# A graph network with two residual norms on one core: loads, split order and product order at both ends changed

## The chip, the cores and the metric

One core of one Trainium2 chip. The metric is the device time of one execution in microseconds (us); lower is better.

## The reference

16 independent batches, each with node features x (512 x 256) and a weighted adjacency adj (512 x 512), all float32:

```python
x = layernorm(x + (adj @ (x @ W0 + b0)) / adj.sum(-1))
y = relu(adj @ (x @ W1) + b1)
y = relu(adj @ (y @ W2) + b2)
out = layernorm(x + adj @ (y @ W3) + b3)
```

The kernel moves b0 behind the division (row sums cancel), so it adds b0 to x ahead of the first sum.

## The kernel before, in words

**Precision.** TensorE works on float32r. Every operand is split in two: `hi` is a rounded copy (by ScalarE, `copy_hi`, line 424), `lo` is full minus hi (by VectorE, `sub_hi`, line 596, or by GpSimd, lines 789, 797, 804). A product is three passes, hi*hi, hi*lo, lo*hi, accumulated in one PSUM bank (`three_passes`, lines 166 to 168). VectorE and ScalarE read the banks; GpSimd reads SBUF alone.

**Tiles.** T = 4 tiles of 128 nodes, KF = 2 halves of 128 features. Eight products make a batch: p0 = x W0 (h), p1 = adj h, then norm1 gives x1; p2 = adj x1 (g, transposed), p3 = g W1 and relu (x2), p4 = x2 W2 (s2), p5 = adj s2 and relu (x3), p6 = x3 W3 (s3), p7 = adj s3, then norm2 gives y and the store. p0, p1, p4, p6 and p7 work tile by tile on 256 columns, p2, p3 and p5 on 512. Four banks are called bank_b (p0, p1, p6, p7), four bank_a.

**Order.** Each engine has its program written out by hand, and semaphores tie them together. An engine runs its own program in order, so what is queued behind a waiting instruction waits too. TensorE interleaves two batches: `step(new)` runs p5(old), p2(new), p6(old), p3(new), p7(old), p0(nxt), p4(new), p1(nxt). The first batch, FIRST, and the first products of `second` stand ahead of the loop; the last step is written out behind it (lines 408 to 419), as LAST and `old`.

**Start.** SyncE's queue (SP) issues every load: w0, xT of batch 0 in two halves, adj of batch 0 in two halves, x, b0; then line 192 waits until both halves of xT are split, because the second batch's xT goes into the same buffer `xT_raw`; then adj of batch 1 in two halves (into `adj_rows`, free then), w1, and behind a wait for xb (line 197) x of batch 1 and the rest. ScalarE's own program for the start is lines 544 to 578, VectorE's 721 to 754, GpSimd's 816 to 829. GpSimd adds b0 to x (`add_b0`, xb), then splits adj of `second`. p1(second) waits for all four h_lo and all four adj_lo of its batch (lines 304, 305). 18 products on zeros (`warm_up`) run before the first load lands.

**End.** VectorE's `norm2(old)` makes, for tile a, v = bank + x1b, its statistics, and for tile a - 1 the reciprocal deviation and y; its first turn waits, at line 685, until the store of the batch before is complete, since `y` is one buffer. `stored` counts 16 for each store. SP stores the last but one batch with line 224 when all its four y are ready, and the last batch tile by tile with line 228.

Of the kernel before, what the change touches and what calls it, by code (L numbers as in the profile page):

```python
# [10 lines left out]
P = 128  # L11
# [8 lines left out]
def build(nc, xT, x, adjT, adj, w0, w1, w2, w3, b0, b1, b2, b3, out):  # L20
# [8 lines left out]
    with ExitStack() as ctx:  # L29
# [7 lines left out]
        xT_raw = sb("xT_raw", [P, T, KF, P], F32)  # L37
# [24 lines left out]
        xT_hi, xT_lo = pair("xT", [P, T, KF, P])  # L62
# [32 lines left out]
        adj1_loaded = [sem(f"adj1_half{n}_loaded") for n in range(2)]  # L95
        rows_loaded = sem("rows_loaded")
# [75 lines left out]

        block = ctx.enter_context(nc.Block())

        @block.sync
        def _(sp):
# [6 lines left out]
            halves = [half_of(half, T) for half in range(2)]  # L183
# [21 lines left out]
            def load(i):  # L205
# [6 lines left out]
                sp.dma_start(xT_raw[:, :], xT[i]).then_inc(xT_loaded, DMA)  # L212
# [19 lines left out]
        def _(pe):  # L232
# [11 lines left out]

            def p0(nxt, reader, read, banks=bank_b):
# [8 lines left out]
                xw_product(p0_done, banks, (lambda k, j: xT_hi[:, j, k, :], lambda k, j: xT_lo[:, j, k, :]), 0, ready)  # L254
# [515 lines left out]
        def _(pool):  # L770
# [98 lines left out]
```

## Time and profile before

| | us |
|---|---|
| three runs: median (lowest, highest) | 555.73 (554.92, 555.89) |
| the profiled execution's own time | 556.23 |
| its span, first to last instruction | 554.4 |
| warm-up products | 1.19 to 4.86 |
| first product of p0 | 5.19 |
| first product of the loop's first step, p5(FIRST) | 43.85 |
| last product of p7(LAST) starts | 549.57 |
| last store issued | 552.18 |

Mean granted TensorE clock over the span 0.996; the core's loads and stores move 58.23 MB at a mean of 105 GB/s, but 316 GB/s between 5 and 10 us. The profile gives for each instruction its start and length from the span's start, and, where its engine was idle before it, for how long and what released it. "x2" joins instructions of one kind: the length is then that of the pair, from the first's start to the last's end.

### The profile page before, as it was taken

Reading aid. Unit: us, or ns where it says so; the run is one execution under the profiler, and the core shown is the slowest. Engines: PE = TensorE matmul, PEld = TensorE weight load, DVE = VectorE, ACT = ScalarE, POOL = GpSimd, SP = SyncE. Lnnn points to the kernel's source line nnn. Section 1 sums busy time; section 2 is a strip of 40 time slices with the busy share of each in tenths; the row PEclk is TensorE's granted clock in tenths of the full one; section 3 lists DMA queues with packets and bytes.
Section 4 is the critical chain, followed back from the end, with each engine's and each line's share of the span. In section 5 each row is a group of like instructions: output and inputs, shape, how many; then the busy total and the mean of one; then the engine's idle time right before and its main releaser. Section 6 shows DMA issues by size and latency. Waiting matters only on the chain.

```text
span 554.4 us, 10623 instructions
## 1 busy us (share of the span) xinstructions
PE 540.8 (98%) x3666; PEld 498.8 (90%) x3666; DVE 350.6 (63%) x1034; ACT 307.5 (55%) x757; POOL 207.6 (37%) x223
## 2 busy tenths in 40 slices
PE   7799999999999999999999999999999999999996
PEld 6778999989899898999989899898999989899885
DVE  5774665756657475665756657475665757657455
ACT  4456646566554756655566554746655566553632
POOL 1745409062260804408062260804408062261000
PEclk9899999999999999999999999999999999999999
DMA  7730070511507033070612507043070612500002
GB/s 248 250 128 2 1 267 1 215 53 59 208 0 264 1 121 144 4 260 0 207 57 61 204 0 265 0 136 129 9 256 0 217 49 63 204 2 39 1 1 77
DMA packets 15286, 58.23 MB, mean 105 GB/s; under 512 B 1952, under 2 KB 2720, under 8 KB 13472
## 3 DMA queue, kind: packets, MB, share of 16 engines
q1 hardware_dynamic: 15264, 57.94, 29.1%
q8 instruction: 13, 0.21, 0.2%
q14 instruction: 9, 0.07, 0.0%
HBM read 49.55 MB, written 8.39 MB: 104 GB/s over the span
## 4 chain that ended last, share of the span: by engine, by line
PE 93%; DVE 3%; DMA 2%; ACT 1%; issue 0%; SPq 0%; DVEq 0%
PE bank_a L166 16%; PE bank_a L167 16%; PE bank_a L168 16%; PE bank_b L166 15%; PE bank_b L167 15%; PE bank_b L168 15%; DMA xT_raw<-in_xT 2%; DVE xT_lo L596 0%; DVE x_lo L596 0%; DVE v L645 0%; DVE x L652 0%; DVE stats L656 0%; DVE h_lo L596 0%; ACT x_hi L500 0%; ACT xT_hi L424 0%
## 5 line engine op out<-in xcount | busy, mean ns | idle before, releaser
L797 POOL TENSOR_TENSOR adj_lo<-adj_raw,adj_hi 128x512 fp32r<-128x512 f32 x56 | 70.8, 1299 | 272.5 <-ACT adj_hi L424 272.5
L596 DVE TENSOR_TENSOR x_lo<-bank_a,x_hi 128x512 fp32r<-128x512 f32 x64 | 44.3, 692 | 69.8 <-ACT bank_a L502 69.8
L166 PE MATMUL bank_b<-h_hi,adj_hi 128*128 128x256 f32 (+1 forms) x256 | 72.0, 281 | 3.8 <-DVE h_lo L596 2.6
L166 PE MATMUL bank_b<-s_hi,adj_hi 128*128 128x256 f32 x256 | 71.8, 280 | 0.9 <-DVE s_lo L596 0.9
L167 PE MATMUL bank_b<-h_lo,adj_hi 128*128 128x256 f32 (+1 forms) x256 | 71.8, 280 | 0.0
L477 ACT ACTIVATE std<-moments,eps_col 128x1 f32<-128x1 f32 x64 | 18.9, 295 | 95.2 <-DVE moments L664 95.2
L168 PE MATMUL bank_b<-h_hi,adj_lo 128*128 128x256 f32 (+1 forms) x256 | 71.6, 279 | 0.0
L167 PE MATMUL bank_b<-s_lo,adj_hi 128*128 128x256 f32 x256 | 71.4, 279 | 0.0
L168 PE MATMUL bank_b<-s_hi,adj_lo 128*128 128x256 f32 x256 | 71.4, 279 | 0.0
L500 ACT ACTIVATE x_hi<-bank_a,b_col 128x512 fp32r<-128x512 f32 x64 | 43.8, 684 | 22.4 <-PE bank_a L168 20.9
L784 POOL TENSOR_TENSOR x1b<-x,b_all 128x256 f32<-128x256 f32 x64 | 46.2, 763 | 17.4 <-DVE x L652 17.4
L166 PEld LDWEIGHTS bank_b<-h_hi,adj_hi 128*128 128x128 f32 x256 | 48.3, 189 | 4.6 <-DVE h_lo L596 2.8
L778 POOL TENSOR_TENSOR xb<-x_raw,b_all 128x256 f32<-128x256 f32 x64 | 47.0, 776 | 13.0 <-DMA b_all<-in_b 11.6
L166 PE MATMUL bank_a<-adj_hi,x_hi 128*128 128x512 f32 x128 | 50.6, 395 | 0.2 <-DVE x_lo L596 0.2
L167 PE MATMUL bank_a<-adj_lo,x_hi 128*128 128x512 f32 x128 | 50.3, 393 | 0.0
L168 PE MATMUL bank_a<-adj_hi,x_lo 128*128 128x512 f32 x128 | 50.2, 392 | 0.0
L521 ACT ACTIVATE std<-moments,eps_col 128x1 f32<-128x1 f32 x64 | 18.9, 295 | 56.2 <-DVE moments L704 56.2
L167 PE MATMUL bank_a<-adj_lo,s_hi 128*128 128x512 f32 x128 | 49.9, 390 | 0.0
L166 PE MATMUL bank_a<-adj_hi,s_hi 128*128 128x512 f32 x128 | 49.9, 390 | 0.0
L168 PE MATMUL bank_a<-adj_hi,s_lo 128*128 128x512 f32 x128 | 49.9, 389 | 0.0
L166 PEld LDWEIGHTS bank_b<-s_hi,adj_hi 128*128 128x128 f32 x256 | 48.1, 188 | 1.8 <-DVE s_lo L596 1.1
L167 PEld LDWEIGHTS bank_b<-s_lo,adj_hi 128*128 128x128 f32 x256 | 47.9, 187 | 0.7
(95 smaller groups left out, 1596.8 us busy)
## 6 DMA issues: line engine op xcount, KB each, us to landing
adj_raw<-in_adjT SPq DMA_DIRECT2D x30, 512.0 KB, 5.6
adj_rows<-in_adj SPq DMA_DIRECT2D x14, 1024.0 KB, 9.4
x_raw<-in_x SPq DMA_DIRECT2D x16, 512.0 KB, 7.4
xT_raw<-in_xT SPq DMA_DIRECT2D x15, 512.0 KB, 6.6
out_y<-y SPq DMA_DIRECT2D x15, 512.0 KB, 2.9
w_raw<-in_w SPq DMA_DIRECT2D x4, 256.0 KB, 5.0
adj_rows<-in_adjT SPq DMA_DIRECT2D x2, 512.0 KB, 7.8
xT_raw<-in_xT SPq DMA_DIRECT2D x2, 256.0 KB, 4.3
```

The source lines that it names most:

```text
L166: pe.matmul(acc, st[0], mv[0], start=start, stop=False)
L167: pe.matmul(acc, st[0], mv[1], start=False, stop=False)
L168: return pe.matmul(acc, st[1], mv[0], start=False, stop=stop)
L477: act.activation(std1[:, j:j + 1], moments1[:, j, 1:2], ACT.Sqrt, bias=eps_col[:, :]).then_inc(std1_ready, 1)
L500: act.activation(hi[:, f, :], bank_a[f][:, :], ACT.Relu, bias=bias[:, f:f + 1])
L521: act.activation(std2[:, j:j + 1], moments2[:, j, 1:2], ACT.Sqrt, bias=eps_col[:, :]).then_inc(std2_ready, 1)
L596: return dve.tensor_tensor(lo, full, hi.bitcast(F32), ALU.subtract)
L778: pool.tensor_tensor(xb[:, j, :], x_raw[:, j, :], b0_all[:, :], ALU.add).then_inc(xb_ready, 1)
L784: pool.tensor_tensor(x1b[:, slot(batch), j, :], x1[:, j, :], b3_all[:, :], ALU.add).then_inc(x1b_ready, 1)
L797: pool.tensor_tensor(adj_lo[:, s, k, :], raw[:, k, :], adj_hi[:, s, k, :].bitcast(F32), ALU.subtract).then_inc(adj_split, 1)
```

## The change

Start:
- ScalarE's queue issues the four adj transfers of batches 0 and 1, at the head of its program; SP keeps the rest.
- xT and x of batch 1 go into the buffers `y` and `v2`, so SP's waits of lines 192 and 197 are gone. `xT_raw` is laid out as [P, T, F], the same bytes in the same order.
- adj of batch 0 is split by two engines: GpSimd takes k = 0 and 2, VectorE 1 and 3.
- ScalarE's, VectorE's and GpSimd's orders are changed to fit: norm1(FIRST, tile 0) stands ahead of both splits of the second xT on VectorE.

End:
- TensorE's order is p3, p7(old, 0 and 1), p4, p5, p7(old, 2), p6, p7(old, 3), p7. p7(old, 2) and (old, 3) write bank_a. `p6_last` runs the half k = 0 over all four tiles, then k = 1.
- s3 of LAST goes into the buffers of h, so that p7(old) can still read s3 of `old`.
- GpSimd makes y of tiles 0 to 2 of LAST. Line 685's wait stays as it is, and GpSimd has the same one.

The diff, cut to its core:

```diff
             sp.dma_start(w_raw[:, 0, :, :], w0).then_inc(w_loaded[0], DMA)
-            for half, tiles in enumerate(halves):
-                sp.dma_start(xT_raw[:, tiles], xT[0, :, tiles]).then_inc(xT0_loaded[half], DMA)
-            for half, tiles in enumerate(halves):
-                sp.dma_start(adj_raw[:, tiles, :], adjT[0, :, tiles, :]).then_inc(adj_loaded[half], DMA)
+            for half in range(2):
+                tiles = half_of(half, T)
+                sp.dma_start(xT_raw[:, tiles, :], xT[0, :, tiles, :]).then_inc(xT0_loaded[half], DMA)
             sp.dma_start(x_raw[:, :, :], x[0]).then_inc(x_loaded, DMA)
             sp.dma_start(b0_all[:, :], b0.partition_broadcast(P)).then_inc(b_loaded[0], DMA)
-
-            sp.wait_ge(xT_split, 2)
-            sp.dma_start(xT_raw[:, :], xT[1]).then_inc(xT_loaded, DMA)
-            for half, tiles in enumerate(halves):
-                sp.dma_start(adj1_raw[:, tiles, :], adjT[1, :, tiles, :]).then_inc(adj1_loaded[half], DMA)
+            sp.dma_start(xT1_raw[:, :, :], xT[1]).then_inc(xT_loaded, DMA)
             sp.dma_start(w_raw[:, 1, :, :], w1).then_inc(w_loaded[1], DMA)
-            sp.wait_ge(xb_ready, T)
-            sp.dma_start(x_raw[:, :, :], x[1]).then_inc(x_loaded, DMA)
+            sp.dma_start(x1_raw[:, :, :], x[1]).then_inc(x1_loaded, DMA)
...
@@ TensorE
-                pe.wait_ge(s2_split, at(old, T, T))
                 adj_product_T(old, p5_done, bank_a[0:2], (s2_hi, s2_lo), s2_split)
...
+            def p6_last(old):
+                for k in range(KF):
+                    pe.wait_ge(x3_split, at(LAST, KF, k + 1))
+                    for j in range(T):
+                        cols = slice(j * P, (j + 1) * P)
+                        if k == 0 and j < T // 2:
+                            pe.wait_ge(v2_ready, at(old, T, j + 1))
+                        mm = three_passes(pe, bank_b[j][:, 0:F], (x3_hi[:, k, cols], x3_lo[:, k, cols]),
+                                          (w_hi[:, 3, k, :], w_lo[:, 3, k, :]), k == 0, k == KF - 1)
+                        if k == KF - 1:
+                            mm.then_inc(p6_done, 1)
...
             p4(LAST)
-            p7(old, range(2, 3))
             p5(LAST)
-            p7(old, range(3, T))
-            p6(LAST, v2_ready, old)
+            p7(old, range(2, 3), bank_a)
+            p6_last(old)
+            p7(old, range(3, T), bank_a)
             p7(LAST)
@@ ScalarE
+            for batch, raw, loaded in ((0, adj_raw, adj_loaded), (1, adj1_raw, adj1_loaded)):
+                for half in range(2):
+                    tiles = slice(half * T // 2, (half + 1) * T // 2)
+                    act.dma_start(raw[:, tiles, :], adjT[batch, :, tiles, :]).then_inc(loaded[half], DMA)
             act.wait_ge(eps_set, 1)
             act.activation(sqrt_eps[:, :], eps_col[:, :], ACT.Sqrt)
             split_xT(FIRST, 0)
+            split_adj(FIRST, 0)
             split_xT(FIRST, 1)
+            split_adj(FIRST, 1)
             h(FIRST, tiles=range(0, 2))
-            split_adj(FIRST, 0)
-            split_adj(FIRST, 1)
-            h(FIRST, tiles=range(2, T))
             split_adj(FIRST, 2)
             split_adj(FIRST, 3)
+            h(FIRST, tiles=range(2, T))
+            split_adj(second, 0)
+            split_adj(second, 1)
             split_xT(second, 0)
             split_xT(second, 1)
-            split_adj(second, 0)
-            split_adj(second, 1)
             norm1(FIRST, None, range(0, 1))
...
             s2(LAST)
-            norm2(before(LAST), range(2, 3))
             x3(LAST, 0)
             x3(LAST, 1)
+            norm2(before(LAST), range(2, 3))
+            s3(LAST)
             norm2(before(LAST), range(3, T))
-            s3(LAST)
             norm2(LAST)
@@ VectorE
             split_xT(FIRST, 0)
             split_xT(FIRST, 1)
+            split_adj0(1)
             h(FIRST, tiles=range(0, 2))
-            split_adj(FIRST, 0)
-            split_adj(FIRST, 1)
+            split_adj0(3)
             h(FIRST, tiles=range(2, T))
-            split_adj(FIRST, 2)
-            split_adj(FIRST, 3)
+            norm1(FIRST, range(0, 1))
             split_xT(second, 0)
-            norm1(FIRST, range(0, 1))
             split_xT(second, 1)
             norm1(FIRST, range(1, 2))
...
             s2(LAST)
-            norm2(before(LAST), range(2, 3))
             x3(LAST, 0)
             x3(LAST, 1)
-            norm2(before(LAST), range(3, T + 1))
+            norm2(before(LAST), range(2, 3), bank_a)
             s3(LAST)
+            norm2(before(LAST), range(3, T + 1), bank_a)
             norm2(LAST)
@@ GpSimd
+            for k in range(0, T, 2):
+                pool.wait_ge(adj_hi_ready, k + 1)
+                pool.tensor_tensor(adj_lo[:, 0, k, :], adj_raw[:, k, :], adj_hi[:, 0, k, :].bitcast(F32),
+                                   ALU.subtract).then_inc(adj0_even_split, 1)
             pool.wait_ge(b_loaded[0], DMA)
             add_b0(FIRST)
...
+            pool.wait_ge(stored, at(LAST, DMA, DMA))
+            for j in range(T - 1):
+                pool.wait_ge(rstd2_ready, at(LAST, T, j + 1))
+                pool.tensor_scalar(y[:, j, :], v2[:, j, :], moments2[:, j, 0:1], rstd2[:, j:j + 1],
+                                   ALU.subtract, ALU.mult).then_inc(y_last_ready, 1)
```

## Rows read from the trace of the kernel before

**Rows 1.** The page, busy time of each engine (share of the span)
```profile
PE 540.8 (98%) x3666; PEld 498.8 (90%) x3666; DVE 350.6 (63%) x1034; ACT 307.5 (55%) x757; POOL 207.6 (37%) x223
```

**Rows 2.** Stretches: length; busy PE, PEld, DVE, ACT, POOL; clock; DMA share; GB/s
```profile
20.00:25.00 5.00, 2.36 (x19) 2.17 (x18) 3.92 (x13) 1.69 (x6) 5.00 (x6) 0.96 0.73 219
25.00:30.00 5.00, 4.84 (x16) 3.62 (x16) 4.29 (x13) 2.14 (x6) 3.62 (x5) 0.70 0.80 289
```

**Rows 3.** TensorE's timeline at the start: start, length, instruction, [idle before <-releaser]
```profile
1.19 3.67 PE L260 MATMUL bank_a<-zeros 128*128 128x256 f32 x18 [1.19 <-DVE zeros L721]
...
10.71 0.36 PE L166 MATMUL bank_b<-h_hi,adj_hi 128*128 128x258 f32 x1 [0.76 <-DVE adj_lo L596]
...
23.48 0.39 PE L166 MATMUL bank_b<-h_hi,adj_hi 128*128 128x258 f32 x1 [2.64 <-DVE h_lo L596]
```

**Rows 4.** VectorE's timeline at the start
```profile
15.89 0.69 DVE L596 TENSOR_TENSOR xT_lo<-xT_raw,xT_hi 128x512 fp32r<-128x512 f32 x1 [2.31 <-ACT xT_hi L424]
16.50 0.16 DVE L635 RECIPROCAL inv_rows<-bank_b 128x1 f32<-128x1 f32 x1
...
17.93 1.22 DVE L596 TENSOR_TENSOR xT_lo<-xT_raw,xT_hi 128x512 fp32r<-128x512 f32 x1
```

**Rows 5.** ScalarE's timeline at the start
```profile
7.35 0.63 ACT L424 ACTIVATE xT_hi<-xT_raw 128x512 fp32r<-128x512 f32 x1 [2.31 <-DMA xT_raw<-in_xT]
...
9.21 1.15 ACT L424 ACTIVATE adj_hi<-adj_raw 128x512 fp32r<-128x512 f32 x2 [0.68 <-DMA adj_raw<-in_adjT]
10.27 0.64 ACT L424 ACTIVATE h_hi<-bank_b 128x256 fp32r<-128x256 f32 x2
```

**Rows 6.** TensorE's timeline at the end
```profile
530.95 0.28 PE L166 MATMUL bank_b<-s_hi,adj_hi 128*128 128x256 f32 x1
...
539.99 0.38 PE L166 MATMUL bank_b<-w_hi,x_hi 128*128 128x256 f32 x1 [0.64 <-DVE x_lo L596]
...
543.93 0.39 PE L166 MATMUL bank_b<-s_hi,adj_hi 128*128 128x256 f32 x1 [0.93 <-DVE s_lo L596]
```

**Rows 7.** VectorE's timeline at the end
```profile
527.47 0.42 DVE L688 TENSOR_TENSOR v<-bank_b,x1b 128x256 f32<-128x256 f32 x1
...
528.55 0.39 DVE L688 TENSOR_TENSOR v<-bank_b,x1b 128x256 f32<-128x256 f32 x1
...
530.53 1.46 DVE L596 TENSOR_TENSOR s_lo<-bank_a,s_hi 128x256 fp32r<-128x256 f32 x4 [0.64 <-ACT s_hi L424]
...
545.75 0.42 DVE L688 TENSOR_TENSOR v<-bank_b,x1b 128x256 f32<-128x256 f32 x1 [1.87 <-PE bank_b L168]
...
549.89 0.42 DVE L688 TENSOR_TENSOR v<-bank_b,x1b 128x256 f32<-128x256 f32 x1
...
551.74 0.41 DVE L698 TENSOR_SCALAR y<-v,moments,rstd 128x256 f32<-128x256 f32 x1
```

**Rows 8.** GpSimd's timeline at the start
```profile
12.08 3.50 POOL L778 TENSOR_TENSOR xb<-x_raw,b_all 128x256 f32<-128x256 f32 x4 [11.62 <-DMA b_all<-in_b]
17.30 5.50 POOL L797 TENSOR_TENSOR adj_lo<-adj_rows,adj_hi 128x512 fp32r<-128x512 f32 x4 [1.72 <-ACT adj_hi L424]
```

**Rows 9.** Issues of w0 and x0: size each, us from issue to landing; SyncE's timeline
```profile
w_raw<-in_w SPq DMA_DIRECT2D x1, 256.0 KB, 2.8
...
3.21 0.43 SPq L189 DMA_DIRECT2D x_raw<-in_x  x1
...
x_raw<-in_x SPq DMA_DIRECT2D x1, 512.0 KB, 8.5
```

**Rows 10.** Table of half microseconds at the start
```profile
2.50:3.00 0.50, 0.50 (x4) 0.50 (x4) 0.00 (x0) 0.00 (x0) 0.00 (x0) 1.00 0.95 356
4.50:5.00 0.50, 0.37 (x4) 0.16 (x2) 0.32 (x1) 0.50 (x1) 0.00 (x0) 1.00 1.10 119
```

**Rows 11.** SyncE's timeline and the DMA issues at the end
```profile
542.14 0.35 SPq L224 DMA_DIRECT2D out_y<-y  x1
...
out_y<-y SPq DMA_DIRECT2D x1, 512.0 KB, 2.6
```

More of the change, by code:

```diff
@@ L60, in build @@
         std1 = sb("std1", [P, T], F32)
-        xT_hi, xT_lo = pair("xT", [P, T, KF, P])
+        xT_hi, xT_lo = pair("xT", [P, T, F])
         g_hi, g_lo = pair("g", [P, KF, N])
@@ L171, in build @@
         adj1_raw = adj_rows
+        xT1_raw, x1_raw = y, v2
+        s3_last_hi, s3_last_lo = h_hi[:, :, 0:F], h_lo[:, :, 0:F]
         block = ctx.enter_context(nc.Block())
@@ L252, in ready @@
                         pe.wait_ge(reader, at(read, T, j + 1))
-                xw_product(p0_done, banks, (lambda k, j: xT_hi[:, j, k, :], lambda k, j: xT_lo[:, j, k, :]), 0, ready)
+                xw_product(p0_done, banks, (features(xT_hi), features(xT_lo)), 0, ready)
             def warm_up():
@@ L360, in p6, with p7 @@
                            lambda j: pe.wait_ge(reader, at(read, T, j + 1)))
-            def p7(old, tiles=range(T)):
+            def p6_last(old):
[9 more added lines that the diff above has]
+                            mm.then_inc(p6_done, 1)
+            def p7(old, tiles=range(T), banks=bank_b):
                 pe.wait_ge(s3_split, at(old, T, T))
+                hi, lo = (s3_last_hi, s3_last_lo) if old is LAST else (s3_hi, s3_lo)
                 s = slot(old)
@@ L600, in split_xT, with split_adj0 @@
                 dve.wait_ge(xT_hi_ready, at(nxt, 2, half + 1))
-                sub_hi(xT_lo[:, tiles], xT_raw[:, tiles], xT_hi[:, tiles]).then_inc(xT_split, 1)
-            def split_adj(nxt, k):
-                s = slot(nxt)
-                dve.wait_ge(adj_hi_ready, at(nxt, T, k + 1))
-                sub_hi(adj_lo[:, s, k, :], adj_raw[:, k, :], adj_hi[:, s, k, :]).then_inc(adj_split, 1)
+                raw = xT1_raw if nxt is second else xT_raw
+                sub_hi(xT_lo[:, tiles, :], raw[:, tiles, :], xT_hi[:, tiles, :]).then_inc(xT_split, 1)
+            def split_adj0(k):
+                dve.wait_ge(adj_hi_ready, k + 1)
+                sub_hi(adj_lo[:, 0, k, :], adj_raw[:, k, :], adj_hi[:, 0, k, :]).then_inc(adj_split, 2)
             def h(new, banks=bank_b, tiles=range(T)):
@@ L676, in x3, with norm2 @@
                 sub_hi(x3_lo[:, f, :], bank_a[f][:, :], x3_hi[:, f, :]).then_inc(x3_split, 1)
-            def norm2(old, turns=range(T + 1)):
+            def norm2(old, turns=range(T + 1), banks=bank_b):
                 for j in turns:
@@ L695, in norm2 @@
                         dve.bn_stats(stats2[:, a, :], v2[:, a, :]).then_inc(stats2_ready, 1)
-                    if b >= 0:
+                    if b >= 0 and (old is not LAST or b == T - 1):
                         dve.wait_ge(rstd2_ready, at(old, T, b + 1))
@@ L771, in add_b0 @@
             def add_b0(batch):
-                pool.wait_ge(x_loaded, at(batch, DMA, DMA))
+                if batch is FIRST:
+                    pool.wait_ge(x_loaded, DMA)
+                elif batch is second:
+                    pool.wait_ge(x1_loaded, DMA)
+                else:
+                    pool.wait_ge(x_loaded, at(batch, DMA, 0))
+                raw = x1_raw if batch is second else x_raw
                 for j in range(T):
@@ L848 @@
     arrays = {
[L849 removed]
+        "xT": x.reshape(NB, P, T, KF, P).transpose(0, 4, 2, 3, 1).reshape(NB, P, T, F),
         "x": x.reshape(NB, P, T, F),
```

46 lines of the change are left out of this document (29 added, 17 removed).

## The prediction

> **What bounds the kernel now.** The page's first part says TensorE: busy 98% of the span [rows 1]. In the middle nothing else can be bought, because TensorE has no gaps there, and the change leaves the loop alone. So I looked for the idle 2% where the change works, at the two ends, first in the table of stretches, then in TensorE's timeline with the idle time before each instruction.
>
> At the start TensorE is busy 2.36 of the 5 us from 20 to 25, and in the next 5 us it is "busy" but at a mean clock of 0.70 [rows 2]. The timeline has the main hole: 2.64 us before 23.48, the first product of the second batch's p1, released by the h_lo split on VectorE [rows 3]. The first p1 starts at 10.71, after 0.76 us of waiting. Following VectorE back from 23.48: it stood 2.31 us until 15.89 for the second batch's xT, which could only be loaded after the first had been split, although p1 of tile 0 was long done; then come norm1 from 16.50 and the second xT split at 17.93, which takes 1.22 us beside a busy GpSimd against 0.69 us for the same shape without one [rows 4]. From VectorE's 16.50 to TensorE's 23.48 it is one chain, 6.98 us. Before it lies the landing of the first xT's second half: ScalarE starts on it at 7.35 [rows 5].
>
> At the end TensorE stands 0.64 us before p6(LAST), for x3's split, and 0.93 us before p7(LAST), for s3's [rows 6]. Then a tail: the last v starts at 549.89, the last y at 551.74 and ends at 552.15 [rows 7], then the last store.
>
> **Start, part by part.** I count everything from L, the moment ScalarE gets xT's second half (7.35 now), because ScalarE runs in order and has that split ahead of split_adj(1) and h.
>
> ScalarE after L: xT_hi, adj_hi 1, h_hi 0 and 1. A pair of adj_hi took 1.15 us and a pair of h_hi 0.64 [rows 5], so adj_hi 1 ends at L+1.15 and h_hi 1 at L+1.8. VectorE: xT_lo to L+1.35, adj_lo 1 to L+1.95, h_lo 0 and 1 (0.37 each) to L+2.7. p1 starts at L+2.75; now it is L+3.36. k=0 and 1 are 12 products of 0.12 us, to L+4.2. For k=2 VectorE first has adj_lo 3, which now has GpSimd's adj_lo 2 beside it, so 1.22 us, then h_lo 2: L+4.5. p1 of tile 0 is done and seen at L+5.9, and norm1(FIRST, 0) can start, since xT1 no longer stands ahead of it. That replaces 16.50. The rest is the chain of 6.98 us plus one more xT split of 1.13 us (both now lie behind norm1). So p1(second) starts at L+14.0; now it is L+16.1. **The new order is worth 2.1 us if L does not move.** Behind it VectorE's chain to x_lo carries p2_first as today, so I let the 2.1 us through whole. Removing the halves of the clock (0.50 in part of that 0.70 stretch) brings nothing of itself: p2 waits for x_lo then.
>
> GpSimd must not be the new end: adj_lo 0 and 2 at about 1.3 us each, done by L+3.7; then four xb in 3.5 and four adj_lo in 5.5 [rows 8], to L+12.7, under L+14.0, if b0 has landed by L+5. Loads of w1, w2, w3 and x1 come earlier on SP; nobody waits on them. Four issues on ScalarE's queue cost it 4 x 0.43 us, before anything is there to split: hidden by the first xT's landing (4.4 now), and the table load moves behind them under the same cover. The other format of xT changes no run of bytes: a partition still reads one contiguous piece.
>
> **But L moves.** Today w0 and both xT halves, 0.79 MB, are first in one queue; w0 lands 2.8 us after its issue [rows 9]. Now four adj transfers of 0.52 MB are issued on a second queue from 0.75 us on, before or beside w0. No row shows two queues in flight, so I bound it. Lower end: xT keeps its place, L = 7.35, no cost. Upper end: the two queues alternate transfer by transfer at today's pace. Then 2.36 MB go by before xT's second half is in (adj 0.52, w0 0.26, adj 0.52, xT 0.26, adj 0.52, xT 0.26). Exactly 2.36 MB go by today up to x0, and x0, issued at 3.21, takes 8.5 us, landing at 11.7 [rows 9]: L later by 4.4. Between them: today's pace contains poor half-microseconds (119 GB/s at 4.5) beside good ones (356 GB/s at 2.5) [rows 10], and a second queue may fill the poor ones. 2.36 MB at 356 are 6.6 us, from first bytes at about 2.0, and w0 shows 0.9 us from its last byte to its landing: 9.5, so L later by 2.2. I take this value: alternation seems the natural thing for two queues on the same engines, and today's stalls look like waiting rather than limit. **Start: -2.1 + 2.2 = +0.1** (from -2.1 to +2.3).
>
> The Trainium skill, "DMA: Bandwidth & Descriptors", in "Queues, rings and completion order", says that each engine takes turns between its queue rows, a packet at a time, and its rules for authors say that spreading transfers over SP, ACT and GpSimd gives no bandwidth. That speaks against this half of the change, and by it alone the upper bound, alternation at an unchanged pace, would be the sum; no run here shows it.
>
> **End, part by part.** p7(old, 2) at 530.95 is moved behind p5(LAST). s2's splits run from 530.53 at 0.37 us each [rows 6, 7], so p5 starts at 531.0 without a hole. x3 is then split 1.3 us earlier (538.6) while p7(old, 2) and the first half of p6_last (12 + 12 products) keep TensorE busy to 539.2; p7(old, 3) covers s3's split (12 products, 1.41 us, against 1.1). Both holes go: 0.64 and 0.93, and 0.1 each because the product behind a hole takes 0.39 and not 0.28. p7(LAST) starts at 542.1 instead of 543.93, **1.8 us earlier for TensorE**. Other banks (bank_a 2 and 3) are free by then.
>
> What is queued behind? norm2(old, 3) now comes after p7(old, 3), at 542.1. v to y is one chain of 2.26 us (549.89 to 552.15), so with 0.3 us from product to v, y of the last but one batch is whole at 544.65. Today its store is issued at 542.14 [rows 11]. That store took 2.6 us, so it lands at 547.3 instead of 544.7. And norm2(LAST), line 685, waits for `stored` before its first v. Today that v comes at 545.75, held by TensorE, with the store in already. **Now it is held by the store, 1.5 us later than today.** Then VectorE works through four turns that TensorE has ready: 527.47 to 528.55 is 1.08 us a turn, with rstd in it about 1.16, where today TensorE paces them at 1.42. The last v starts at 550.8 against 549.89; the last y saves 0.15 because y 2 is on GpSimd. **End: +0.75** (from +0.4 to +1.0). GpSimd's tensor_scalar has no row; by its 128x256 tensor_tensor (0.8 us) y 2 is done at 552.0, before VectorE's y 3 at 552.9, and hidden; at twice that it would still be level.
>
> **Sum.** +0.1 + 0.75 = +0.85. The profiled execution took 556.23 (span 554.4, 1.8 around it); the median is 555.73, so I subtract 0.5: 555.73 + 0.85 = 556.6. A measurement of this kernel can tell about 0.2%, 1.1 us, from no change.
>
> **Rivals.**
> 1. *xT is not delayed.* For: ScalarE's first issue may come late (behind its table load, 1.28 us), and SP's three transfers are small. Against: adj's are issued within the same microsecond. -2.1 + 0.75 = -1.35, 554.4. Decides if L stays below 7.8. Chance 0.22.
> 2. *Strict alternation at today's pace.* +2.3 + 0.75 = +3.05, 558.8: slower. For: 2.36 MB have a landing today. The taking of turns that the Trainium skill describes in "DMA: Bandwidth & Descriptors" would be this case. Chance 0.2.
> 3. *The clock falls early.* The warm-up ends at 4.86 [rows 3]; if xT comes late, TensorE idles about 3 us, and today 2.64 us of idle is followed by the level 1.2 GHz [rows 2, 3]. Half speed under p1_first costs up to 1.5 us more: 558.1. Chance 0.12.
> 4. *The wait for the store does not bind* (y whole earlier than I count): -1.8 and +0.1 give 554.0, with rival 1 551.8. Against: the order of VectorE's program is fixed. Chance 0.08.
> The forecast keeps 0.38.
>
> **Numbers.** Faster by over 0.2%: most of rivals 1 and 4, 0.27. Slower: rivals 2 and 3 and some of the forecast's upper side, 0.41. Within: 0.32. The range holds rivals 1 and 2 and half of 4's spread: 553.6 to 559.2. The forecast's own range is 555.6 to 557.8.
>
> **What would show it.** Right: xT's second half landing near 9.5; VectorE's norm1 ahead of the second xT split; p1(second) about 14 us after L; no idle before p6 and p7(LAST); VectorE's first v of LAST waiting for out_y's DMA, and turns of 1.1 us behind it. Wrong: xT landing at 7.3 or 11.7, a clock of 0.5 before 15 us, GpSimd's adj_lo releasing p1(second), or v of LAST released by TensorE.

## The result: slower, and the profile after

| | before | after |
|---|---|---|
| median (lowest, highest), us | 555.33 (554.91, 555.89) | 560.0 (559.36, 560.46) |
| span of the profiled execution | 554.4 | 558.3 |
| mean granted clock | 0.996 | 0.991 |
| ScalarE takes xT's second half (L) | 7.35 | 10.90 |
| p1(second) starts | 23.48 | 26.07 |
| p7(LAST) starts | 543.93 | 544.77 |
| first v of LAST | 545.75 | 549.99 |
| last y ends | 552.15 | 555.66 |

The ratio of after to before is 1.008, 95% interval 1.0065 to 1.0096. The forecast was 556.6, range 553.6 to 559.2: the sign it gave most weight to was right, the size was not. Between the two profiled executions the span grows by 3.9 us: the start brings 2.6 and the end the rest. The medians are 4.7 us apart, because the profiled execution of the kernel before (556.23) was 0.9 above its median and that of the kernel after (560.09) only 0.1 above its own.

The first part of the page after, which answers to [rows 1]: the busy times hardly moved, so the change is in what lies between the instructions.

```profile
PE 541.0 (97%) x3666; PEld 500.4 (90%) x3666; DVE 349.7 (63%) x1029; ACT 307.0 (55%) x757; POOL 213.8 (38%) x228
```

**Start.** ScalarE's timeline after (its own DMA issues, then what it split) answers to [rows 5]:

```profile
0.74 0.87 ACTq L571 DMA_DIRECT2D adj_raw<-in_adjT  x2
1.64 1.29 ACTq L571 DMA_DIRECT2D adj_rows<-in_adjT  x2
...
8.97 0.63 ACT L446 ACTIVATE xT_hi<-xT_raw 128x512 fp32r<-128x512 f32 x1 [4.51 <-DMA xT_raw<-in_xT]
...
10.90 0.63 ACT L446 ACTIVATE xT_hi<-xT_raw 128x512 fp32r<-128x512 f32 x1 [0.78 <-DMA xT_raw<-in_xT]
```

adj is issued at 0.74, ahead of w0 at 0.87 on SyncE's queue, and both halves of xT are waited for: L is 10.90, 3.55 us later. The table of stretches shows what the memory gave meanwhile (columns as in [rows 2], which are of later stretches):

```profile
2.00:3.00 1.00, 1.00 (x6) 1.00 (x6) 0.00 (x0) 0.04 (x1) 0.00 (x0) 1.00 0.84 193
3.00:4.00 1.00, 1.00 (x7) 1.00 (x6) 0.00 (x0) 1.00 (x1) 0.00 (x0) 1.00 0.89 250
...
5.00:6.00 1.00, 0.41 (x2) 0.11 (x1) 0.00 (x0) 0.00 (x0) 0.00 (x0) 1.00 1.04 414
```

The two queues reach 414 GB/s together, but only from 5 us on; from 2 to 4 us there were 193 and 250. The profile's DMA view parts the queues (q1 is SyncE's, q10 ScalarE's; packets, MB, share of the 16 engines), here from 3.0 to 3.4, from 3.4 to 3.9 and from 5 to 8 us:

```profile
q10 hardware_dynamic: 23, 0.09, 75.4%
...
q10 hardware_dynamic: 30, 0.12, 94.4%
q1 hardware_dynamic: 8, 0.02, 8.4%
...
q10 hardware_dynamic: 224, 0.84, 72.4%
q1 hardware_dynamic: 189, 0.35, 30.6%
```

Until 3.5 us only adj's queue moved anything, although w0 had been issued at 0.87. From then on the two took packets in about equal numbers (364 on SyncE's queue and 342 on ScalarE's from 4 to 9 us), but SyncE's packets were about half as large here, so w0 and xT got 0.68 MB in that time and adj 1.21. VectorE and TensorE then, against [rows 3] and [rows 4]:

```profile
6.22 0.43 DVE L760 CAST w_hi<-w_raw 128x512 fp32r<-128x512 f32 x1 [4.93 <-DMA w_raw<-in_w]
...
17.30 0.17 DVE L665 RECIPROCAL inv_rows<-bank_b 128x1 f32<-128x1 f32 x1 [1.12 <-PE bank_b L171]
...
18.73 3.01 DVE L624 TENSOR_TENSOR xT_lo<-y,xT_hi 128x512 fp32r<-128x512 f32 x2
...
24.60 1.42 DVE L624 TENSOR_TENSOR h_lo<-bank_a,h_hi 128x256 fp32r<-128x256 f32 x4 [0.94 <-ACT h_hi L446]
```

```profile
9.74 0.77 PE L274 MATMUL bank_b<-w_hi,xT_hi 128*128 128x256 f32 x2 [4.34 <-ACT xT_hi L446]
...
15.90 0.39 PE L169 MATMUL bank_b<-h_hi,adj_hi 128*128 128x258 f32 x1 [0.43 <-DVE h_lo L624]
...
26.07 0.46 PE L169 MATMUL bank_b<-h_hi,adj_hi 128*128 128x258 f32 x1 [2.60 <-DVE h_lo L624]
```

norm1(FIRST, 0) is at L+6.4 where it was at L+9.15, so the order did what it says. But the hole before p1(second) is as wide as before (2.60 for 2.64), and both splits of the second xT, 3.01 us, now stand in the chain ahead of it. Counted from L, p1(second) came at 15.17 where it came at 16.1.

**End.** TensorE's two holes of [rows 6] are gone, and p7(LAST) starts at 544.77, which is the forecast's 542.1 and the start's delay of 2.6:

```profile
540.68 0.28 PE L169 MATMUL bank_b<-w_hi,x_hi 128*128 128x256 f32 x1
...
544.77 0.34 PE L169 MATMUL bank_b<-h_hi,adj_hi 128*128 128x256 f32 x1
```

What stands in their place is in VectorE's, GpSimd's and SyncE's timelines, against [rows 7] and [rows 11]:

```profile
546.83 0.41 DVE L729 TENSOR_SCALAR y<-v,moments,rstd 128x256 f32<-128x256 f32 x1
549.99 0.42 DVE L718 TENSOR_TENSOR v<-bank_b,x1b 128x256 f32<-128x256 f32 x1 [2.76 <-DMA out_y<-y]
...
551.08 0.39 DVE L718 TENSOR_TENSOR v<-bank_b,x1b 128x256 f32<-128x256 f32 x1
...
555.13 0.53 DVE L729 TENSOR_SCALAR y<-v,moments,rstd 128x256 f32<-128x256 f32 x1
```

```profile
551.88 3.63 POOL L879 TENSOR_SCALAR y<-v,moments,rstd 128x256 f32<-128x256 f32 x3 [34.22 <-DVE rstd L722]
```

```profile
547.26 0.35 SPq L224 DMA_DIRECT2D out_y<-y  x1
553.13 3.21 SPq L231 DMA_DIRECT2D out_y<-y  x4
```

VectorE stands 2.76 us for the store of the last but one batch, which is issued when its y is whole. While it stands, TensorE runs ahead: the four turns behind it are VectorE's own, 1.1 us apart. GpSimd's three y take 1.2 us each, end at 555.51, 0.15 before VectorE's last, and so leave two stores to issue behind the end in place of one.

### The profile page after: what moved, and what is told of

Read it like the earlier page. It is cut to its first block, busy times and chain, and to the rows that moved or that the text cites. A ratio compares the mean times of both kernels' runs of the same rounds, so it can differ in the third digit from the quotient of the medians.

```text
span 558.3 us, 10616 instructions
## 1 busy us (share of the span) xinstructions
PE 541.0 (97%) x3666; PEld 500.4 (90%) x3666; DVE 349.7 (63%) x1029; ACT 307.0 (55%) x757; POOL 213.8 (38%) x228
## 4 chain that ended last, share of the span: by engine, by line
PE 91%; DVE 3%; DMA 2%; issue 1%; ACT 1%; POOL 1%; SPq 0%; DVEq 0%; POOLq 0%
PE bank_a L169 16%; PE bank_a L171 16%; PE bank_a L170 16%; PE bank_b L169 15%; PE bank_b L170 15%; PE bank_b L171 15%; DMA xT_raw<-in_xT 1%; DVE xT_lo L624 1%; DMA out_y<-y 0%; POOL adj_lo L853 0%; DVE v L675 0%; DVE x L682 0%; DVE stats L725 0%; POOL xb L813 0%; DVE x_lo L624 0%
## 5 line engine op out<-in xcount | busy, mean ns | idle before, releaser
L169 PE MATMUL bank_b<-h_hi,adj_hi 128*128 128x256 f32 (+1 forms) x272 | 76.7, 282 | 3.0 <-DVE h_lo L624 3.0
L170 PE MATMUL bank_b<-h_lo,adj_hi 128*128 128x256 f32 (+1 forms) x272 | 76.6, 282 | 0.0
L171 PE MATMUL bank_b<-h_hi,adj_lo 128*128 128x256 f32 (+1 forms) x272 | 76.3, 281 | 0.0
L169 PE MATMUL bank_b<-s_hi,adj_hi 128*128 128x256 f32 x232 | 65.0, 280 | 0.0
L170 PE MATMUL bank_b<-s_lo,adj_hi 128*128 128x256 f32 x232 | 64.7, 279 | 0.0
L171 PE MATMUL bank_b<-s_hi,adj_lo 128*128 128x256 f32 x232 | 64.7, 279 | 0.0
L169 PEld LDWEIGHTS bank_b<-h_hi,adj_hi 128*128 128x128 f32 x272 | 51.6, 190 | 3.5 <-DVE h_lo L624 3.4
L170 PEld LDWEIGHTS bank_b<-h_lo,adj_hi 128*128 128x128 f32 x272 | 51.6, 190 | 0.1
L171 PEld LDWEIGHTS bank_b<-h_hi,adj_lo 128*128 128x128 f32 x272 | 51.6, 190 | 0.0
L624 DVE TENSOR_TENSOR g_lo<-bank_a,g_hi 128x512 fp32r<-128x512 f32 x32 | 22.1, 692 | 40.2 <-ACT g_hi L446 40.2
```

What stands on the lines that cost most here:

```text
L169: pe.matmul(acc, st[0], mv[0], start=start, stop=False)
L170: pe.matmul(acc, st[0], mv[1], start=False, stop=False)
L171: return pe.matmul(acc, st[1], mv[0], start=False, stop=stop)
L624: return dve.tensor_tensor(lo, full, hi.bitcast(F32), ALU.subtract)
```

## The experiments

Every run is compared with the kernel before on the same chip; the kernel before had medians of 554.8 to 555.4 there, with single executions from 553.5 to 557.6. Its first loads land at varying times: in four profiled executions with its order of loads ScalarE took xT's second half at 7.35, 6.33, 7.10 and 6.53, and in the three of them with its whole start p1(second) came at 23.48, 22.50 and 22.68. So the profiled execution of the kernel before is a late one. In the six traces with all of adj on ScalarE's queue, L was 10.85 to 11.15 each time.

### Each end by itself

The changed start with the end of before, and the reverse: the parts of the diff swapped whole.

> The start of the change, with the end of the kernel before (order of products, banks, all y on VectorE, each line as before). Theory (the delayed xT at the start costs 2.6 us and passes whole to the end, the end costs 1.3 more): p1 of the second batch starts at 26.1 as in the changed kernel, p7 of the last batch at 546.6 (543.93 + 2.6), span 557.0, ratio 1.0047. Rival (the loop absorbs part of the late start, and the loss lies in the end): p7 of the last batch before 545.5, span near 555.5.

> The start of the kernel before, with the end of the change. Theory (the wait for the last but one store takes the place of the two holes): p1 of the second batch at 23.5, p7 of the last batch at 542.1, first v of the last batch at 547.3, released by the store's DMA, last y done at 553.0, and one more issue of 0.35 us on SyncE's queue behind GpSimd's y 2: span 555.7, ratio 1.0023. Rival (the holes taken away reach the end): first v released by TensorE at 543.9, last y done at 550.3, span 552.6.

The start alone: 558.25, ratio 1.0061 (1.0035 to 1.0087), span 557.2, p1(second) at 26.08 and p7(LAST) at 546.69, as the theory had it: the loop absorbs nothing of the late start. The end alone: 557.48, ratio 1.0039 (1.002 to 1.0058). Its profiled execution had an early start (p1(second) at 22.50, span 554.6), so its end is read from there. VectorE:

```profile
546.27 0.42 DVE L709 TENSOR_TENSOR v<-bank_b,x1b 128x256 f32<-128x256 f32 x1 [2.74 <-DMA out_y<-y]
...
551.40 0.53 DVE L720 TENSOR_SCALAR y<-v,moments,rstd 128x256 f32<-128x256 f32 x1
```

With 0.98 added to bring p1(second) to 23.48, the last y ends at 552.9, 0.76 later than in the kernel before: the forecast's +0.75. Both ends cost, and their sum, 1.0%, agrees with the whole, 0.8%, within the intervals. The ratio of the end alone is larger than its expected 1.0023, which is still inside its interval.

### The end: the wait for the store, and GpSimd's y

The y of LAST goes into the buffer v1, and VectorE and GpSimd no longer wait for the store (cut to its core):

```diff
+        y_last = v1
...
-                sp.dma_start(out[NB - 1, :, j, :], y[:, j, :]).then_inc(stored, DMA)
+                sp.dma_start(out[NB - 1, :, j, :], y_last[:, j, :]).then_inc(stored, DMA)
...
-                        dve.wait_ge(stored, at(old, DMA, DMA))
+                        if old is not LAST:
+                            dve.wait_ge(stored, at(old, DMA, DMA))
...
-            pool.wait_ge(stored, at(LAST, DMA, DMA))
```

> The changed kernel with y of the last batch written into the buffer v1, which is dead by then, so that nothing of the last batch waits for the store of the batch before; GpSimd still makes y 0 to 2. Theory (that wait costs the end): first v of the last batch at 546.5, released by TensorE; last v at 550.75, last y done at 553.0, span 555.9, 2.4 us under the changed kernel. Rival (GpSimd's y at 1.2 us each is the other bound): y 2 comes from GpSimd behind VectorE's y 3, and the span falls by less than 1.5 us.

556.51, ratio 1.0035 (1.0016 to 1.0054), span 555.4, 2.9 below the changed kernel's, with p1(second) at 26.13. The first v of LAST follows VectorE's last y of `old` at once:

```profile
547.18 0.42 DVE L721 TENSOR_TENSOR v<-bank_b,x1b 128x256 f32<-128x256 f32 x1
```

The wait is what the end loses: with it gone, the changed end costs nothing more (against the changed start with the old end, 558.25, this run is 1.7 faster). The first v came 0.7 later than expected, because VectorE was not free earlier. The other suspect, with the wait kept:

```diff
-                    if b >= 0 and (old is not LAST or b == T - 1):
+                    if b >= 0:
...
-            for j in range(T - 1):
-                pool.wait_ge(rstd2_ready, at(LAST, T, j + 1))
-                pool.tensor_scalar(y[:, j, :], v2[:, j, :], ...)
```

> The changed kernel with GpSimd's y of tiles 0 to 2 of LAST given back to VectorE; the buffer and the wait for the store stay. Theory (GpSimd's 1.2 us for each y and the extra issue behind it cost what they save): first v of LAST near 549.9 as in the changed kernel, turns of 1.1, 1.3 and 1.3 us, last y ends 5.9 us after the first v starts, 555.8, and the last store is issued 0.36 us behind it: span equal to the changed kernel's within 0.2, time 560.0. Rival (GpSimd's y is a gain, as it takes 0.4 us a turn off VectorE): time 0.5 to 0.8 us longer than the changed kernel's, 560.6.

559.55, ratio 1.0073 (1.0054 to 1.0092). The profiled execution started late (p1(second) at 27.51); from the first v to the last y's end it is 5.90 us, and SyncE ends 0.36 behind that:

```profile
551.41 0.42 DVE L714 TENSOR_TENSOR v<-bank_b,x1b 128x256 f32<-128x256 f32 x1 [2.88 <-DMA out_y<-y]
...
556.90 0.41 DVE L725 TENSOR_SCALAR y<-v,moments,rstd 128x256 f32<-128x256 f32 x1
```

In the changed kernel the same two are 5.67 and 0.68 (SyncE's last issue ends at 556.34). GpSimd's share gains 0.23 in the turns and gives 0.32 back at the issue of the stores: no difference that can be told, as expected (the ratios are 1.0073 and 1.008).

### The start: which queue, and ScalarE's order

Adj back on SyncE's queue, adj of batch 0 behind xT and adj of batch 1 behind the second xT, all else as changed (in brief; the loops over the halves are left out):

```diff
-            for batch, raw, loaded in ((0, adj_raw, adj_loaded), (1, adj1_raw, adj1_loaded)):
-                ... act.dma_start(raw[:, tiles, :], adjT[batch, :, tiles, :])
+                sp.dma_start(adj_raw[:, tiles, :], adjT[0, :, tiles, :]).then_inc(adj_loaded[half], DMA)
...
+                sp.dma_start(adj1_raw[:, tiles, :], adjT[1, :, tiles, :]).then_inc(adj1_loaded[half], DMA)
```

> The changed kernel with the four adj loads back on SyncE's queue (w0, xT, adj of batch 0, x, b0, xT of batch 1, adj of batch 1, w1 and so on, no waits), nothing else. Theory (the second queue makes xT late): xT's halves land at 4.4 and 7.3; but ScalarE now has adj 0's split ahead of xT's second split, so it stands until adj lands at 9.2 and takes xT's second half at 9.8; p1 of the second batch at 24.9, 1.2 us earlier than in the changed kernel, span 557.1. Rival (the engines are slow at first whoever issues): xT's second half lands near 10.9 and p1 of the second batch stays at 26.1.

559.25, ratio 1.0087 (1.0056 to 1.0117), p1(second) at 25.84, where 24.9 was expected: a miss. ScalarE's part came as expected. The second half of xT had landed at about 5.9, and ScalarE stood at adj, which its new program has in front:

```profile
9.21 0.63 ACT L452 ACTIVATE adj_hi<-adj_raw 128x512 fp32r<-128x512 f32 x1 [4.29 <-DMA adj_raw<-in_adjT]
9.74 0.61 ACT L452 ACTIVATE xT_hi<-xT_raw 128x512 fp32r<-128x512 f32 x1
```

What was late is what followed: norm1(FIRST, 0) came 7.2 us behind L and not 6.4, for VectorE's split of that half took twice its time beside GpSimd's adj_lo, and TensorE waited 0.66 us more for it and then ran most of p0's second half at 0.63 us a pair, where the full clock gives 0.40.

```profile
10.39 1.36 DVE L626 TENSOR_TENSOR xT_lo<-xT_raw,xT_hi 128x512 fp32r<-128x512 f32 x1 [4.75 <-ACT xT_hi L452]
```

So the queue and ScalarE's order belong together, and this run tells neither from the other. Two more tried parts of it. Only adj of batch 1 back on SyncE's queue:

```diff
+                sp.dma_start(adj1_raw[:, tiles, :], adjT[1, :, tiles, :]).then_inc(adj1_loaded[half], DMA)
...
-            for batch, raw, loaded in ((0, adj_raw, adj_loaded), (1, adj1_raw, adj1_loaded)):
...
+                act.dma_start(adj_raw[:, tiles, :], adjT[0, :, tiles, :]).then_inc(adj_loaded[half], DMA)
```

> The changed kernel with only adj of batch 0 on ScalarE's queue; adj of batch 1 goes back to SyncE's, behind xT of batch 1. Now 1.83 MB instead of 2.36 MB go by before xT's second half is in. Theory (alternation transfer by transfer at some 400 GB/s): xT's second half is taken at 9.6 instead of 10.9, p1 of the second batch starts at 24.8, span 557.0. Rival (the delay comes from two queues as such, not from the bytes ahead): xT's second half stays at 10.9, p1 at 26.1.

559.17, ratio 1.0071 (1.0051 to 1.0092). ScalarE takes xT's second half at 9.27, 1.6 us earlier, so the bytes ahead of it count, as the theory says; half of the gain arrives in the profile, and none that can be told in the median:

```profile
8.21 0.63 ACT L449 ACTIVATE xT_hi<-xT_raw 128x512 fp32r<-128x512 f32 x1 [5.07 <-DMA xT_raw<-in_xT]
...
9.27 0.61 ACT L449 ACTIVATE xT_hi<-xT_raw 128x512 fp32r<-128x512 f32 x1
```

```profile
25.30 0.39 PE L169 MATMUL bank_b<-h_hi,adj_hi 128*128 128x258 f32 x1 [2.19 <-DVE h_lo L626]
```

Here all twelve pairs of p0's products took 0.63 us or more; in the changed kernel it was six, and the rest took 0.39 to 0.47.

And the clock: 40 warm-up products in place of 18 (`WARM`).

> The changed kernel with 40 warm-up products instead of 18, so that TensorE works on until about 9.4, when the first xT half is split. Theory (the granted clock fell to 0.50 from about 9.4 to 12.3 because TensorE had idled 4.3 us, and p0 at half speed holds h by 0.4 us): clock 1.00 from 9 to 13 us, p0's products of 0.28 us instead of 0.63, p1 of the second batch at 25.6 instead of 26.1, span 557.9. Rival (the fallen clock is hidden behind ScalarE's and VectorE's splits): p1 of the second batch stays at 26.0 or later.

558.93, ratio 1.0068 (1.0048 to 1.0089), p1(second) at 25.65, L at 10.97. The stretch from 11 to 12 us, in the changed kernel and in this one (the figure before the DMA share is the granted clock):

```profile
11.00:12.00 1.00, 1.00 (x6) 1.00 (x6) 0.44 (x1) 1.00 (x3) 0.48 (x1) 0.50 1.06 399
```

```profile
11.00:12.00 1.00, 0.99 (x9) 0.78 (x7) 0.36 (x1) 1.00 (x2) 0.54 (x1) 1.00 1.02 372
```

The clock of 1.2 GHz under p0, after 4.34 us without a product, cost 0.4 us at p1(second), as expected: small, and in the medians not to be told. Next, one queue with ScalarE's xT splits in front of adj, so that neither is late:

```diff
             split_xT(FIRST, 0)
-            split_adj(FIRST, 0)
             split_xT(FIRST, 1)
+            split_adj(FIRST, 0)
             split_adj(FIRST, 1)
```

> The changed kernel with two things undone at the start: all adj loads back on SyncE's queue, and ScalarE splits both xT halves before adj 0 and 1. Theory (the late xT costs, the order itself is sound): ScalarE takes xT's second half by 6.0 to 7.3, adj_hi 0 at 9.2 when adj lands, first product of p1 at 11.8, norm1(FIRST, 0) near 15.3, and from there the 8.8 us that the changed kernel shows to p1(second): 24.1. Span 556.3, about 2.0 below the changed kernel, time 558.0. Rival (the new order itself costs, since TensorE's wait for adj's splits halves its clock under p1 of FIRST whatever the queue): clock 0.5 between 11 and 15, p1(second) at 25 or later, span 557.3, as the run with one queue and the change's order showed (25.84).

559.2, ratio 1.0064 (1.0045 to 1.0082), span 557.5: the rival. xT's second half was taken at 6.89 and p1(second) still came at 25.34.

```profile
12.54 0.36 PE L169 MATMUL bank_b<-h_hi,adj_hi 128*128 128x258 f32 x1 [3.03 <-DVE h_lo L626]
...
25.34 0.39 PE L169 MATMUL bank_b<-h_hi,adj_hi 128*128 128x258 f32 x1 [2.58 <-DVE h_lo L626]
```

```profile
16.69 0.17 DVE L667 RECIPROCAL inv_rows<-bank_b 128x1 f32<-128x1 f32 x1 [2.57 <-PE bank_b L171]
...
18.12 2.88 DVE L626 TENSOR_TENSOR xT_lo<-y,xT_hi 128x512 fp32r<-128x512 f32 x2
```

With one queue the new order loses at both of its places: h waits behind adj's splits, and ScalarE gets adj at about 9.2, so p1 starts only at 12.54 and runs at half the clock from 13.4 to 16.7 (its products then take 0.42 us for 0.28); then both xT splits stand in a row.

### The parts one at a time, with the end of before

First the buffers alone: second xT and x in `y` and `v2`, SyncE's two waits gone, one queue, every order as before.

> The kernel before with one part of the change: the second xT and x in the buffers of y and v2 and SyncE's two waits gone; one queue, the orders of all engines and the whole end as before. Theory (of the 1.9 us that buffers and better end gave together against before, 1.4 were the end's): p1(second) at 22.1, norm1(FIRST, 0) near 15.3, holes of 0.64 and 0.93 back, time 0.5 below the kernel before, ratio 0.999. Rival A (the wait on SyncE was the start's hole): 1.4 us below, ratio 0.9975. Rival B (earlier traffic of the second xT takes from adj of batch 0 what it gives): no difference.

554.98, ratio 0.9988 (0.9975 to 1.0001), p1(second) at 22.37: it agrees with the theory's half microsecond, but the interval also holds no change, and rival A at its other end. In its profiled execution xT's first half was late (taken at 5.97) and p0 ran mostly at the 1.2 GHz level. To that run one part each was added. On VectorE, norm1(FIRST, 0) ahead of both xT splits:

```diff
-            split_xT(second, 0)
             norm1(FIRST, range(0, 1))
+            split_xT(second, 0)
             split_xT(second, 1)
```

> The run with the buffers alone (one queue, orders and end of the kernel before) and one edit on VectorE: norm1(FIRST, 0) ahead of both splits of the second xT, as the change has it. Theory (the reordering costs, as it puts both splits, 1.1 to 1.45 us each beside GpSimd's adj_lo, between two turns of norm1, while TensorE's p1 of tile 0 lets norm1 start only 0.2 us earlier): norm1 at 15.4 where it was 15.55, then 8.1 to 8.7 us: p1(second) at 23.5 to 24.1 against 22.37, time 1.1 to 1.7 above the run with the buffers alone (554.98), near 556.4. Rival (the forecast's step: norm1 gains what the split ahead of it took): p1(second) within 0.3 of 22.37, time unchanged.

555.25, ratio 0.9999 (0.9985 to 1.0013). The theory, a cost of 1.1 to 1.7, falls; the rival stands, no difference that can be told. The profiled execution was 1.2 us below its median (554.06), so its p1(second) at 21.51, 0.86 ahead of the run with the buffers alone, is not the order's gain by itself. GpSimd began on adj at 15.88, 1 us after the pair of xT splits, and the pair took 1.61 us. From norm1 to p1(second) it is 8.06 us, the forecast's 8.1:

```profile
13.45 0.17 DVE L659 RECIPROCAL inv_rows<-bank_b 128x1 f32<-128x1 f32 x1 [0.90 <-PE bank_b L169]
...
14.89 1.61 DVE L618 TENSOR_TENSOR xT_lo<-y,xT_hi 128x512 fp32r<-128x512 f32 x2
```

```profile
21.51 0.36 PE L167 MATMUL bank_b<-h_hi,adj_hi 128*128 128x258 f32 x1 [2.11 <-DVE h_lo L618]
```

The other half, adj's splits ahead of h and two of the four on GpSimd:

```diff
             split_xT(FIRST, 1)
-            h(FIRST, tiles=range(0, 2))
             split_adj(FIRST, 0)
             split_adj(FIRST, 1)
+            h(FIRST, tiles=range(0, 2))
@@ VectorE
+            split_adj0(1)
             h(FIRST, tiles=range(0, 2))
-            split_adj0(0)
-            split_adj0(1)
+            split_adj0(3)
```

> The run with the buffers alone and the other half of the change's order: GpSimd splits adj of batch 0 for k = 0 and 2, and both engines have the first adj splits ahead of h; VectorE's norm1(FIRST, 0) stays between the splits of the second xT. Theory (h behind adj waits for adj's landing near 9.2, TensorE stands about 3 us and its clock is 0.5 under p1 of FIRST): first product of p1 at 12.5, norm1(FIRST, 0) at 16.7 as in the run with one queue and xT first, then 6.9 us: p1(second) 23.6, 1.2 above the buffers alone, time 556.2. Rival (the second engine on the first split pays): norm1 at or before 15.5 and p1(second) at or below 22.4.

555.81, ratio 1.0004 (0.999 to 1.0019). TensorE stands 2.29 us before its first p1 product, at 12.65, and p1(second) is at 24.14, 0.5 beyond the theory and 1.8 beyond the run with the buffers alone; in the median it is 0.8, with intervals that overlap. The second engine on the first split pays nothing. Neither half of the order by itself loses the 3.0 us by which p1(second) is later in the run with one queue and xT first (25.34 against 22.37): there norm1(FIRST, 0) came 1.1 us later, and from it to p1(second) it was 8.65 us in place of 6.82.

Last the second queue by itself: adj's four transfers on ScalarE's queue, every order as before.

> The run with the buffers alone and adj's four transfers issued on ScalarE's queue, as the change has them; orders and end as in the kernel before. This puts L late as in the changed kernel (10.9) with the old order. Forecast's step (the new order is worth 2.1 at a given L): p1(second) at L + 16.1 or later, 27.0 to 28.2, against the changed kernel's 26.07. Theory now (with adj landed early the new order is worth at most 1 us): p1(second) near L + 15.6, 26.5. Rival (the new order costs here too, as it does with one queue): 24.5 to 25.5. Span from p1(second): 553.3 + (p1(second) - 22.37), so 557.4 by the theory; time 559.1.

558.64, ratio 1.0054 (1.004 to 1.0068), near the theory's 26.5 and 559.1. ScalarE, VectorE and TensorE:

```profile
10.85 0.63 ACT L438 ACTIVATE xT_hi<-xT_raw 128x512 fp32r<-128x512 f32 x1 [1.33 <-DMA xT_raw<-in_xT]
```

```profile
19.17 0.17 DVE L657 RECIPROCAL inv_rows<-bank_b 128x1 f32<-128x1 f32 x1 [0.18 <-PE bank_b L169]
```

```profile
9.66 0.77 PE L269 MATMUL bank_b<-w_hi,xT_hi 128*128 128x256 f32 x2 [4.26 <-ACT xT_hi L438]
10.23 0.63 PE L272 MATMUL bank_b<-w_lo,xT_hi 128*128 128x256 f32 x2
...
26.27 0.39 PE L167 MATMUL bank_b<-h_hi,adj_hi 128*128 128x258 f32 x1 [1.17 <-DVE h_lo L616]
```

This settles the start's larger part. The queue alone moves the median by 558.64 - 554.98 = 3.7 us against the buffers alone and p1(second) by 3.9. And at the same L as the changed kernel (10.85 and 10.90) the old order reaches p1(second) at 26.27, the new one at 26.07.

### A version that beats both

One queue, the buffers, the start's old orders; at the end the change's product order and banks, y of LAST in v1, no wait for the store and no y on GpSimd. And the same end on the start of before.

> Start: one queue in the order w0, xT, adj of batch 0, x, b0, xT of batch 1, adj of batch 1, w1, x of batch 1, all without a wait, the second xT and x in the buffers y and v2; ScalarE's, VectorE's and GpSimd's orders as in the kernel before. End: the change's products and banks, but y of the last batch in v1 and all of it made by VectorE, without the wait for the store. Theory: xT's second half at 5.9 to 7.3; the second xT lands near 13.0 and VectorE's split of it starts at 13.7 instead of 15.9, p1 of the second batch at 21.9 (now 23.5); no idle of VectorE for a store at the end, last y 1.8 us earlier against TensorE's frame: span 551.0, ratio 0.994. Rival (contention of the earlier second xT with adj of batch 0, or GpSimd's adj splits become the bound): p1 of the second batch at 23 or later, span over 552.3.

> Start: the kernel before, line for line. End: the change's products and banks, y of the last batch in v1, all made by VectorE, no wait for the store. Theory (the two holes are worth 1.8 us once nothing waits for the store): p7 of the last batch at 542.1 in the frame of before (1.8 us nearer to the start of the loop), last v released by TensorE, last y done at 550.3, span 552.6, ratio 0.9967. Rival (VectorE, behind with norm2 of the batch before, holds the end instead): last v later than TensorE's last product by more than 0.5 us, gain under 1 us.

553.3, ratio 0.9966 (0.9954 to 0.9979), and 553.71, ratio 0.9975 (0.996 to 0.9989); the two can't be told apart. Counted from p1(second) to the end of the span, TensorE's 1.8 us arrive, or nearly: 529.1 us on the start of before and 529.3 with the buffers, where the kernel before needs 530.9. The medians gain less than the 0.9967 and 0.994 expected, since those were counted from the late profiled execution of the kernel before. VectorE in the first of the two:

```profile
543.19 0.42 DVE L715 TENSOR_TENSOR v<-bank_b,x1b 128x256 f32<-128x256 f32 x1
...
548.68 0.41 DVE L726 TENSOR_SCALAR v<-v,moments,rstd 128x256 f32<-128x256 f32 x1
```

## Why the prediction was wrong, step by step

**The end's mechanism was right.** "Now it is held by the store": first v at 547.3 + 2.67 (p7(LAST) 544.77 against 542.1) = 549.97, measured 549.99; last y +0.75, measured +0.84 after taking off the same 2.67. Short was GpSimd's tensor_scalar: taken at 0.8 us by its tensor_tensor, it takes 1.2. It stays hidden as a computation, as the bound said, but the store behind it does not: SyncE's last issue ends 0.68 behind the last y, where it was 0.37. **+0.3 that had no term.**

**L was mis-sized.** "L later by 2.2": it was 3.55, inside the bounds of 0 and 4.4 but nearer to the upper one. "I take this value: alternation" of whole transfers at 356 GB/s from 2.0 us on, and 0.9 us to land, is the step that failed, in three parts. The pace: 2.36 MB had moved at about 9.0 (the stretches of 1 us from 2.0 to 9.0 sum to 2.34 MB), not at 8.6. The turns: SyncE's queue moved nothing before 3.5 us and then took turns by packets, of which its own were the smaller ones, so w0 and xT, 0.79 MB, were through only at about 9.7, when adj's queue had moved 1.9 MB and not 1.57. The landing: from there to ScalarE's start at 10.90 it is 1.2 us, where the forecast allowed 0.9, read from w0 at the head of the only queue. **1.35 us in all**, as an estimate from these times about 0.4, 0.7 and 0.3. The Trainium skill, "DMA: Bandwidth & Descriptors", "Queues, rings and completion order", says that an engine takes turns between queue rows a packet at a time. From 4 to 9 us the trace agrees (364 and 342 packets); what held w0 back before 3.5 us it doesn't explain: w0, 0.26 MB and issued at 0.87, landed behind adj's first half, 5.3 us after its issue instead of 2.8. The Trainium skill's rule on the same page, in "Rules for kernel authors", that more queues give no bandwidth is not borne out in bytes: from 2 to 9 us two queues moved 2.34 MB, one queue 2.05 MB in the run with the buffers alone. For xT it holds all the same, since the extra bytes were adj's.

**The order was over-rated.** "The new order is worth 2.1 us if L does not move." At L near 10.9 it is worth 0.2 (15.17 against 15.42 behind L), in the medians nothing (1.0061 for the changed start, 1.0054 for the queue alone). The forecast set the new order at L+14.0 against the old kernel's L+16.1. Its parts:
- norm1(FIRST, 0) at L+5.9: it was L+6.4. Of this 0.4 is the clock at 1.2 GHz under p0, shown by the longer warm-up, which was rival 3 at less than a third of its price.
- one more xT split at 1.13: the pair took 3.01 us, 0.75 more than two at 1.13, since both lie beside GpSimd's adj_lo. The one row of such a split at hand (1.22 us) was taken to stand for both, and they took 1.5 each.
- The comparison itself. The old L+16.1 held 2.31 us of waiting for the second xT, which the new buffers cure without any new order: with them and a late L the old order needs L+15.42. Of the 2.1, 0.7 were the buffers' (p0 ran at 0.63 us a pair in both runs at the late L, so the comparison with each other is fair), and after the two mis-sizings nothing much is left for the order.

So the start came to -1.0 + 3.55 = +2.6 where the forecast had -2.1 + 2.2 = +0.1. With the end's 0.84 and 0.3 and 0.1 to 0.2 of small terms, that is the span's 3.9.

**The median was taken over from the kernel before.** The forecast subtracted 0.5, because the profiled execution was above the median. The kernel after has no such gap (560.09 and 560.0): the kernel before is often faster than its profiled execution, by an earlier start (p1(second) at 22.50 and 22.68 in two others), while L at 10.85 to 11.15 came back in every trace with adj on ScalarE's queue. **+0.4.** This also fits the start alone, which cost 3.4 us in the median and 2.6 in the profiled execution.

**The rivals.** Rival 2 (strict alternation at today's pace) was the nearest: its L of 11.7 was 0.8 too late and its order 1.1 too good. The two large errors of the forecast, 1.35 and 1.15, had the same sign, but together they reach 559.1, just inside the range; the 0.3 of the store, 0.1 of the last y and the 0.4 of the median took the time out of it. That the sign was right is partly luck: the end's +0.75 was well founded, the start's +0.1 was a sum of two terms that were both off by more than itself.

**Left open.** Why SyncE's queue moves nothing before 3.5 us when adj is issued beside it was not tried, with other sizes or with adj issued a little later; nor was adj on ScalarE's queue behind xT's landing. The clock's fall under p0 belongs to both runs at the late L: in the run with the queue alone, after 4.26 us without a product, the profile's clock column reads 1.00, but the pairs took 0.63 us as in the changed kernel, after 4.34 us; with the longer warm-up they took 0.40:

```profile
10.31 0.63 PE L277 MATMUL bank_b<-w_lo,xT_hi 128*128 128x256 f32 x2
```

```profile
10.10 0.40 PE L277 MATMUL bank_b<-w_lo,xT_hi 128*128 128x256 f32 x2
```

## What to carry to other kernels

Give a load that the critical chain waits for the queues to itself: here bulk loads issued on a second queue beside it went first and took its bytes, and their early landing bought nothing in return. When work is pulled forward, look which wait on a shared buffer (a store, here) was hidden behind the time that is taken out, and move the buffer with the work. And when several edits reach for the same gap, measure the cheapest alone (the buffers here) before crediting the rest.

## What the runs showed of the hardware

- With adj's 0.52 MB transfers issued first on ScalarE's queue, SyncE's queue moved nothing before 3.5 us (0.02 MB by 4 us), in the changed kernel as in the runs with the start alone and with the queue alone; the total was 193 and 250 GB/s from 2 to 4 us, against 293 and 367 in the run with the buffers alone. From 5 us on the two carried 375 to 414, which one queue reaches as well (406 to 416 from 12 to 15 us in that run). A 0.26 MB load issued 0.1 us behind a 0.52 MB one on the other queue landed 2.5 us later than at the head of the only one.
- GpSimd's tensor_scalar of 128x256 (subtract, multiply, f32) takes 1.2 us, its tensor_tensor of the same shape 0.83; VectorE's tensor_scalar takes 0.41, and 0.53 beside GpSimd's.
- VectorE's 128x512 subtract from SBUF takes 0.69 us alone and 1.4 to 1.5 each in a pair beside GpSimd's adj_lo (3.01 and 2.88 us for two; 2.36 to 3.51 over all runs with the changed start), and 1.61 for the pair where GpSimd was still at rest for part of it.
- An idle of 4.3 us before p0 was followed by the 1.2 GHz level, read from the products themselves (0.63 us a pair, 0.40 with an idle of 1.91 us), also where the profile's clock column stayed at 1.00.
